# One operand of VectorE's long two-input instructions kept in PSUM, in a graph network kernel

## The reference

```
h  = relu(layernorm(x));  h1 = relu(h @ Wp1.T + bp1)
p  = segment_max(h1[src], dst)               # 0 where a node has no edge
x1 = relu([h, p] @ Wm1.T + bm1)              # and twice more with its own pooling, residual and layernorm
x  = x + x3
h  = relu(layernorm(x));  q, k, v = h @ Wq + bq (scaled), h @ Wk + bk, h @ Wv + bv     # 8 heads of 32
s  = sum over d of q[src] * k[dst]           # per edge and head
a  = exp(s - segment_max(s, src)) / segment_sum(...)
x  = x + segment_sum(a * v[dst], src) @ Wo + bo
```

## Time and profile before

| | us |
|---|---|
| median of 3 runs | 6471.6 (6447.24 to 6482.15) |
| the profiled execution | 6475.84 |
| its span on the core | 6474.0 |
| busy: POOL / DVE / PE / ACT | 4276.2 / 3947.8 / 2983.5 / 1424.0 |
| Degrees, Ranks, Permute (stretches read) | 1275, 1360, 1240 |
| attention pass (stretch read) | 1795 |

### The profile page before, as it was taken

The page is one execution under the profiler, slowest core; times in us unless marked ns, Lnnn a source line. Parts: engine busy times, 40 slices in busy tenths (PEclk is TensorE's granted clock), DMA queues, the critical chain, the costliest instruction groups (busy, mean ns, idle before and its releaser), DMA issues. The chain is left out here.

```text
span 6474.0 us, 65110 instructions
## 1 busy us (share of the span) xinstructions
PE 2983.5 (46%) x14550; PEld 1929.9 (30%) x14610; DVE 3947.8 (61%) x7945; ACT 1424.0 (22%) x2231; POOL 4276.2 (66%) x3748
## 2 busy tenths in 40 slices
PE   3222210025555565566777766678333333333335
PEld 3111100013444444444333322245222222222224
DVE  4555655554454555557555655565577777777776
ACT  3000000002111121125666666654000000000001
POOL 1666667755555556655888888840787887888774
PEclk8555555557666666668888888889666666666667
DMA  4444445544444444445555554443566666666663
GB/s 132 151 166 154 159 161 173 171 137 145 140 154 145 154 159 166 167 144 168 170 171 174 178 171 165 165 130 124 161 173 177 175 176 176 175 176 173 178 177 112
DMA packets 339899, 1039.80 MB, mean 161 GB/s; under 512 B 73288, under 2 KB 140576, under 8 KB 306424
## 3 DMA queue, kind: packets, MB, share of 16 engines
q0 software_dynamic: 208656, 615.00, 33.2%
q1 hardware_dynamic: 131176, 424.06, 17.4%
HBM read 652.25 MB, written 386.67 MB: 160 GB/s over the span
## 5 line engine op out<-in xcount | busy, mean ns | idle before, releaser
L480 POOL DMA_INDIRECT G<-tab,ix x2349 | 2647.2, 1127 | 1185.7 <-issue 692.2
L502 DVE SCALAR_TENSOR_TENSOR G<-G,reset 128x256 f32<-128x256 f32 x2349 | 1128.8, 481 | 834.0 <-DMA G<-tab,ix 443.9
L1292 POOL DMA_INDIRECT kv<-kvtab,ix x936 | 1178.8, 1259 | 285.1 <-issue 285.1
L1394 PE MATMUL bank<-kv,ident 128*128 128x264 f32 x1872 | 604.1, 496 | 1208.6 <-DVE kv L1334 592.1
L926 PE MATMUL bank<-signs,work 128*128 128x425 bf16 (+1 forms) x3072 | 823.0, 423 | 384.9 <-DVE work L898 354.8
L912 ACT ACTIVATE signs<-iota,off 128x937 bf16<-128x937 f32 x783 | 802.8, 1071 | 450.2 <-PE bank L926 325.1
L1394 PEld LDWEIGHTS bank<-kv,ident 128*128 128x128 f32 x1872 | 465.4, 254 | 1347.7 <-DVE kv L1334 1049.3
L926 PEld LDWEIGHTS bank<-signs,work 128*128 128x128 bf16 x3132 | 320.9, 111 | 865.2 <-issue 454.2
L1311 DVE TENSOR_TENSOR kv<-kv,q 128x3072 f32<-128x3072 f32 x78 | 262.5, 3366 | 425.2 <-DMA kv<-kvtab,ix 425.2
L1312 DVE TENSOR_REDUCE s<-kv 128x96 f32<-128x3072 f32 x78 | 439.6, 5636 | 2.7
L1379 ACT ACTIVATE w<-w 128x120 f32<-128x120 f32 x78 | 23.6, 303 | 1772.3 <-DVE w L1329 1660.7
(11 more groups left out here) (262 smaller groups left out, 5027.3 us busy)
## 6 DMA issues: line engine op xcount, KB each, us to landing
hist<-G SPq DMA_DIRECT2D x261, 1152.0 KB
G<-tab,ix POOLq DMA_INDIRECT x2349
ahist<-state SPq DMA_DIRECT2D x78, 408.0 KB
tab<-o SPq DMA_DIRECT2D x147, 128.0 KB
kv<-kvtab,ix POOLq DMA_INDIRECT x936
kvtab<-okv SPq DMA_DIRECT2D x49, 260.0 KB
h<-tab SPq DMA_DIRECT2D x98, 128.0 KB
cur<-tab SPq DMA_DIRECT2D x98, 128.0 KB
```

The source lines that it names most:

```text
L480: g.indirect_dma_start(G[b][:, k, :], None, tab, bass.IndirectOffsetOnAxis(ix[:, b, k:k + 1], 0)).then_inc(s_eg[b].sem, 16)
L502: ins = v.scalar_tensor_tensor(out=G[b][:, k, :], in0=before, scalar=reset[:, bass.ds(n * J + k, 1)], in1=G[b][:, k, :], op0=ALU.add, op1= ...
L1292: g.indirect_dma_start(kvs[b][:, k, :], None, kvtab, bass.IndirectOffsetOnAxis(ix[:, b, k:k + 1], 0)).then_inc(s_eg[b].sem, 16)
L1394: m = pe.matmul(ps_row(b, r), ident[:, :], kvs[b][:, r * SLOT + e, D:KV], start=(e == 0), stop=(e == SLOT - 1))
```

## The change

All eight PSUM banks used to be separate tensors. Banks 4, 5 and 6 become one tensor `wide` of 1,536 f32 columns (`bank[4]` to `bank[6]` are slices of it). Then:

- `Degrees`: the iota row is kept in bank 6, as f32, in place of an SBUF tensor in bf16.
- `Permute`: the iota row is kept in bank 6, and `hot`, the one-hot that L891 writes and L898 reads twice, lies over banks 4, 5 and a part of 6, as f32.
- `attention_pass`: ACT gets a second task, `bring`, which copies the batch's three query rows from SBUF into `wide` once they have landed and once the scores of the batch before are made; DVE's multiply reads them there. The query gathers get semaphores of their own. The exponential is written to PSUM (banks 3, 6 and 7 for the three buffers) in place of SBUF, and the weighing and the rescaling read it there. PE's sums use banks 0, 1 and 2 alone, one for each row of the batch, and its wait for DVE's batch counter is dropped, since its wait for the weighing comes behind DVE's reading of the bank.

`Ranks` and the folds are left as they are.

```diff
--- before.py
+++ after.py
@@ -192,7 +192,10 @@
         nmr = sb(top, "nmr", [P, NT])
         rows_upto = sb(top, "rows_upto", [P, NT])
         rows_own = sb(top, "rows_own", [P, NT])
-        bank = [top.enter_context(nc.psum_tensor(f"bank{n}", [P, 512], F32)) for n in range(8)]
+        bank = {n: top.enter_context(nc.psum_tensor(f"bank{n}", [P, 512], F32)) for n in (0, 1, 2, 3, 7)}
+        wide = top.enter_context(nc.psum_tensor("wide", [P, 3 * 512], F32))
+        for n in range(3):
+            bank[4 + n] = wide[:, n * 512:(n + 1) * 512]
 
 
         s_const = sem("s_const")
@@ -646,7 +649,7 @@
                 self.cnt = [sb(st, "cnt", [P, NT]) for _ in range(2)]
                 self.low = [sb(st, "low", [P, J, P], BF16) for _ in range(2)]
                 self.high = [sb(st, "high", [P, J, NT], BF16) for _ in range(2)]
-                self.iota = sb(st, "iota", [P, P], BF16)
+                self.iota = bank[6][:, 0:P]
                 self.lo = [sb(st, "lo", [P, CH], BF16) for _ in range(2)]
                 self.hi = [sb(st, "hi", [P, CH], BF16) for _ in range(2)]
                 self.oh, self.mm, self.added = sem("deg_oh"), sem("deg_mm"), sem("deg_added")
@@ -856,12 +859,12 @@
                 self.row, self.lo, self.hi = (sb(st, n, [P, CH], BF16) for n in ("row", "lo", "hi"))
                 self.off = sb(st, "off", [P, CH])
                 self.iota = sb(st, "iota", [P, SL + 1])
-                self.iotab = sb(st, "iotab", [P, P], BF16)
+                self.iotab = wide[:, 2 * 512 + 2 * P:2 * 512 + 3 * P]
                 self.rows_made, self.signs_made, self.mm = sem("perm_rows"), sem("perm_signs"), sem("perm_mm")
                 self.ready = sem("perm_ready")
                 self.cuts = ((0, 512), (512, SL + 1))
                 self.signs = sb(st, "signs", [P, self.RG, SL + 1], BF16)
-                self.hot = sb(st, "hot", [P, J, P], BF16)
+                self.hot = wide[:, 0:J * P].rearrange("p (k e) -> p k e", e=P)
 
                 work = sb(st, "work", [P, 4 * (SL + 1)])
                 self.vals = work[:, 0:UB * J * P].bitcast(BF16).rearrange("p (b m k e) -> p b m k e", b=UB, m=2, k=J)
@@ -1271,12 +1274,15 @@
             row_max = sb(st, "row_max", [P, R, HEADS])
             w = sb(st, "w", [P, UB, R * SLOT + R, HEADS])
             tmp = sb(st, "tmp", [P, ACC])
-            c_weighted, c_summed = sem("att_weighted"), sem("att_summed")
-            GATHERS = R * SLOT + R
+            c_weighted, c_summed, c_query = sem("att_weighted"), sem("att_summed"), sem("att_query")
+            s_query = [sem(f"att_q{b}") for b in range(UB)]
+            query = wide[:, 0:R * D].rearrange("p (r f) -> p r f", f=D)
+            wts = [bank[n][:, 0:(R * SLOT + R) * HEADS].rearrange("p (k h) -> p k h", h=HEADS) for n in (3, 6, 7)]
+            GATHERS = R * SLOT
             EXPS = R + 1
 
             def ps_row(b, r):
-                return bank[(b * R + r) % 8][:, 0:ACC]
+                return bank[r][:, 0:ACC]
 
             def heads(ap):
                 return ap.rearrange("p (d h) -> p d h", h=HEADS)
@@ -1287,7 +1293,7 @@
                     def gather(i, b):
                         hold(g, "pool", c_eix.sem, c_eix.base + times(i, b, 2))
                         for r in range(R):
-                            g.indirect_dma_start(qs[b][:, r, :], None, qtab, bass.IndirectOffsetOnAxis(ix[:, b, R * SLOT + r:R * SLOT + r + 1], 0)).then_inc(s_eg[b].sem, 16)
+                            g.indirect_dma_start(qs[b][:, r, :], None, qtab, bass.IndirectOffsetOnAxis(ix[:, b, R * SLOT + r:R * SLOT + r + 1], 0)).then_inc(s_query[b], 16)
                         for k in range(R * SLOT):
                             g.indirect_dma_start(kvs[b][:, k, :], None, kvtab, bass.IndirectOffsetOnAxis(ix[:, b, k:k + 1], 0)).then_inc(s_eg[b].sem, 16)
                     staged(g, NBA, UB, [(0, gather)])
@@ -1304,11 +1310,12 @@
 
                     def score(i, b):
                         n = i * UB + b
-                        kv, q, top_m = kvs[b], qs[b], state[b][:, :, ACC:STATE]
+                        kv, top_m = kvs[b], state[b][:, :, ACC:STATE]
+                        v.wait_ge(c_query, times(i, b, 1))
                         v.wait_ge(s_eg[b].sem, s_eg[b].base + (i * (16 * GATHERS) + 16 * GATHERS))
                         v.wait_ge(s_hs[b].sem, s_hs[b].base + i * 16)
                         keys = kv[:, :, 0:D].rearrange("p (r e) f -> p r e f", e=SLOT)
-                        chain.link(v.tensor_tensor(keys, keys, q[:, :, None, :].to_broadcast([P, R, SLOT, D]), ALU.mult))
+                        chain.link(v.tensor_tensor(keys, keys, query[:, :, None, :].to_broadcast([P, R, SLOT, D]), ALU.mult))
                         chain.link(v.tensor_reduce(s[:, :, :, :].rearrange("p r e h -> p (r e) h"),
                                                    kv[:, :, 0:D].rearrange("p k (d h) -> p k h d", h=HEADS), AX.X, ALU.add))
                         flat = s[:, :, :, :].rearrange("p r e h -> p (r e) h")
@@ -1331,7 +1338,7 @@
 
                     def weigh(i, b, r):
                         vals = kvs[b][:, r * SLOT:(r + 1) * SLOT, D:KV].rearrange("p e (d h) -> p e d h", h=HEADS)
-                        v.tensor_tensor(vals, vals, w[:, b, r * SLOT:(r + 1) * SLOT, None, :].to_broadcast([P, SLOT, ACC // HEADS, HEADS]),
+                        v.tensor_tensor(vals, vals, wts[b][:, r * SLOT:(r + 1) * SLOT, None, :].to_broadcast([P, SLOT, ACC // HEADS, HEADS]),
                                         ALU.mult).then_inc(c_weighted, 1)
 
                     done = [0]
@@ -1344,7 +1351,7 @@
                                     v.wait_ge(c_batch.sem, c_batch.of(i, b - 1, UB))
                             before = state[b][:, r - 1, 0:ACC] if r else state[(b - 1) % UB][:, R - 1, 0:ACC]
                             chain.link(v.tensor_tensor(heads(tmp[:, :]), heads(before),
-                                                       w[:, b, R * SLOT + r, None, :].to_broadcast([P, ACC // HEADS, HEADS]), ALU.mult))
+                                                       wts[b][:, R * SLOT + r, None, :].to_broadcast([P, ACC // HEADS, HEADS]), ALU.mult))
                             ins = v.tensor_tensor(state[b][:, r, 0:ACC], ps_row(b, r), tmp[:, :], ALU.add)
                             if r == R - 1:
                                 ins.then_inc(c_batch.sem, 1)
@@ -1374,20 +1381,20 @@
 
                 @blk.scalar
                 def _(a):
+                    def bring(i, b):
+                        a.wait_ge(s_query[b], i * (16 * R) + 16 * R)
+                        if not is_first(i, b):
+                            a.wait_ge(c_w.sem, c_w.base + times(i, b - 1, EXPS))
+                        a.activation(query, qs[b][:, :, :], ACT.Copy).then_inc(c_query, 1)
+
                     def expo(i, b):
                         a.wait_ge(c_w.sem, c_w.base + times(i, b, EXPS))
-                        a.activation(w[:, b, :, :], w[:, b, :, :], ACT.Exp).then_inc(c_e.sem, 1)
-                    staged(a, NBA, UB, [(0, expo)])
+                        a.activation(wts[b], w[:, b, :, :], ACT.Exp).then_inc(c_e.sem, 1)
+                    staged(a, NBA, UB, [(0, bring), (0, expo)])
 
                 @blk.tensor
                 def _(pe):
                     def add(i, b):
-                        if not is_first(i, b):
-
-                            if b == 0:
-                                pe.wait_ge(c_batch.sem, c_batch.of(i, b - 1, UB))
-                            elif not is_first(i, b, 0, 2):
-                                pe.wait_ge(c_batch.sem, c_batch.of(i, b - 2, UB))
                         for r in range(R):
                             pe.wait_ge(c_weighted, times(i, b, R, r + 1))
                             for e in range(SLOT):
```

## The result

The kernel after took **6944.5 us** (median of 4 runs, 6938.8 to 6954.1) beside 6464.6 us (6447.2 to 6482.2) of the kernel before: a ratio of 1.074, 95% interval 1.071 to 1.078. Forecast were 5930 us, faster; it was slower.

What follows compares the result with a forecast made beforehand. POOL's pace of issuing gathers was taken to bound Permute and attention. From 6475.8 us, 307 (attention), 200 (Permute) and 35 (Degrees) came off, giving 5934, less 4 against the median: 5930 us, range 5860 to 6050.

Steps and rivals of the forecast that it cites:

- Held gathers: Attention and Permute: gathers held by DVE instructions with two SBUF inputs; freeing them wins 307 and 200 us.
- Degrees: Degrees pass: four one-hots a batch read iota from PSUM; at most 104 us, a third taken, 35 us.
- DVE's own time: DVE instructions with PSUM operands, including L891 writing PSUM: no longer, or hidden under POOL's turn; 0 us.
- bring: Attention: ScalarE's copy of query rows to PSUM, at most 1.07 us each, costs nothing; 83 us if exposed.
- the exponential: Attention: exponential into PSUM, PE's three banks and removed wait change nothing, within 78 x 0.1 us either way.
- rival 1: Max passes: PE is starved once gathers flow freely; Degrees and Permute take 15.2 us a batch, 6322 in all; chance 0.2.
- Rival 2: The same PE starvation in attention too, 3.8 us a batch: 6619 us, slower from 3.2 on; chance 0.1.
- The signs it named: Trace marks: POOL waiting for hist stores in Permute (rival 1), for DVE's index copies in attention (Rival 2).
- The base: Whole kernel before: the profiled execution's 6475.8 us, 4 us above the median of 6471.6, from which gains were subtracted.

Runs made afterwards that it cites:

- pause_three: Kernel after plus 3 POOL writes of a scratch tile before each batch's gathers; 6151.9 us, 0.961 of before (6403.0 us there).
- before_pause_three: Kernel before with the same 3 POOL writes before each batch's gathers; 6643.4 us, 1.024 of before (6479.5 us there).
- pause_three_again: Kernel after with 3 POOL scratch writes before each batch's gathers, repeated on another occasion; 5947.0 us, 0.992 of before.

## Why the prediction was wrong

- **Held gathers, found and priced: right.** On a quiet occasion attention gained 313 us (forecast 307), its batch takes 18.8 us (forecast 18.9), its gathers 949 ns. Permute gained 226 us (forecast 200, bound 240), at 11.55 us a batch. This agrees with the rule of the Trainium skill, SBUF — State Buffer, "Who interferes with whom", that the prediction named.
- **Degrees: under-sized, by a misread cause.** 35 us were taken, with the reason "But POOL waits there 165.2 us for stores". On a quiet occasion that wait is 0.3 us, and the gain 106 us, the whole bound of 104. The wait belonged to the disturbance, not to the stage.
- **DVE's own time, `bring`, the exponential: right.** The rows of after, all disturbed, and alike on quiet occasions:

```profile
L894 DVE TENSOR_TENSOR wide<-wide,row 128x1152 f32<-128x1152 f32 x87 | 118.1, 1358 | 1.1 <-issue 1.1
...
L1388 ACT ACTIVATE wide<-q 128x768 f32<-128x768 f32 x78 | 62.6, 802 | 22.5 <-DMA q<-qtab,ix 19.7
...
L674 DVE TENSOR_TENSOR cnt<-bank,cnt 128x49 f32<-128x49 f32 x174 | 28.1, 203 | 612.3 <-remote 596.7 <-issue 15.4
```

  L894, which now writes f32 to PSUM, takes 1.358 us in place of 1.35, the copy of the query rows 0.80. (The last row is for the next point.)
- **The step that failed is the one against rivals 1 and 2.** The forecast put the wait of other engines on PE at nothing in Permute and attention (POOL's turn of 11.4 and 18.9 us was to be the whole batch). Measured it is 6.5 and 3.8 us a batch, and 4.6 in Degrees. The rivals had the mechanism, that what PE delivers comes late once gathers flow freely, and were put down with "nothing says that the gathers' pace is the cause, and Permute's PE, the busiest, has no such wait now". Permute had none *because* its gathers were held. The rows showed the order already: mean hold 73 ns in Ranks, 141 in Degrees, 333 in Permute, and POOL's waits for others 323, 168 and 0 us. The more a pass was held, the less it stalled. That was an order of three passes with different work, a hint and not yet a proof.
- **Rival 2's size.** It borrowed 3.8 us a batch from Ranks and decided from 3.2 on. Measured over the free pace: Degrees 1390 / 87 - 11.4 = 4.6, Permute 6.5, attention 22.7 - 18.9 = 3.8. Its formula with their weighted mean of 5.0, put in after the fact, gives 6475.8 - 4274 + 3458 + 252 x 5.0 = 6920 us; measured 6944.5. It had a chance of 0.1, which was too little: four of the eight occasions were disturbed, the one that the forecast was worked out from among them. The range left it out.
- **The signs it named came.** POOL waits for `hist` stores in Permute (rival 1's) and for the index copies in attention (rival 2's). Of rival 1's picture, single matmuls of PE that go slowly as in Ranks, Permute shows little: there PE stands behind ACT, which learns late of PE's work.
- **The base.** The forecast assumed that 6471.6 us is what the kernel takes. It takes about 6000 us as often, and the sign of the change hangs on which it is. On a quiet occasion the sign of the forecast is right and its size isn't: 641 us gained where 307 + 200 + 35 = 542 were added up, 71 of the difference in Degrees and 26 in Permute. That the time of 5930 us lies between the two measured levels is chance. The trace had a mark of it: idle time put down to "remote" (L765), some 199 us. On a quiet occasion the same row has none, and the 596.7 us of it in L674 above fall to 0.

**What stays open.** What the disturbance is. The runs tell: it comes with an occasion and not with a chip; it delays what comes from PE, more so the more gathers follow each other and the more matmuls PE has; it does not slow the transfers, and halving the gathers' bytes took nothing away in Degrees and Ranks. The disturbed traces also hold far fewer semaphore events, 29,950 in the one of the result and 47,933 in that of before, against 86,883 and 87,073 on quiet occasions; the disturbed runs with three writes lie between, with 43,386 (`pause_three`) and 62,456 (`before_pause_three`). The Trainium skill, NOTIFIC — the notification-queue block, "7.1 Overflow: three behaviours, one of which stalls the engine", says that, when a queue of records is full, a record is dropped, overwrites the oldest or holds up the engine that sends it, by setting; it adds that the marks of such a loss were never seen in its measurements. Lost events and stalls come together here by occasion, but not by stage: between the first and the last gather of Permute of before, disturbed, 7,896 events are left of 17,699 on the quiet occasion, and POOL waits for nobody; in Ranks of `pause_three` 7,429 of the 17,655 of `pause_three_again`, and no stall either. So losing events does not by itself make POOL wait. Whether the way of the records causes the delays no run shows; the one that was to tell met a quiet occasion. Nor can these runs tell whether an execution of which no profile is taken meets the condition at all. Long pauses against evenly spread ones of the same sum were not compared on a disturbed occasion either, so it stays open whether PE's news needs a gap or only fewer gathers in a given time.

## What to carry to other kernels

A stall that hides another one is not pure loss: before you take a wait away, look at a stage of the same kernel that lacks it, and ask why *that* one is slower than its own sum. Where groups of rows on one core name "remote" as the releaser for hundreds of microseconds, the trace may have been taken in a condition that doesn't hold tomorrow; measure the kernel before on several occasions before pricing a change by one. Where a gather flow may meet such a condition, a pause of three such writes a batch on POOL costs a known (5947.0 - 5353.6) / 339 = 1.75 us where nothing is disturbed, and turned 1.055 into 0.961 where it was.

## What the runs showed of the hardware

- A gather beside a DVE instruction with two SBUF inputs is held until that ends; with one operand in PSUM it takes 946 to 949 ns. On a quiet occasion freeing them took 643 us off a span of 5994.
- The same program ran at two levels, 5997 and 6403 us, on one chip on two occasions, each stable within 1.3% over its runs.
- In the disturbed condition matmuls whose recorded end is 5585.80 let DVE go on at 5603.10, and a turn of PE that ended at 3548.06 let ACT go on at 3564.52. Three writes of POOL ahead of each batch of gathers took the whole loss away in Degrees and Ranks (1159 and 1192 us, quiet 1161 and 1192).
- DVE writes 1152 f32 elements to PSUM in 1.358 us, as fast as bf16 to SBUF. ACT copies 768 f32 elements from SBUF to PSUM in 0.80 us.
- POOL starts a gather 0.30 us after a gather, and 0.81 us after a write of its own that it has waited for.
